# Two stages joined into one block, and a four-bit network whose rounding steps are reordered, in an eight-stage transformer kernel

## What is computed

```python
# layer 0, feed-forward: E = 64 experts, H = 32 hidden, G = 64 tokens a group, K = 16
scores = softmax(xt @ Wr + br)                 # T x E
fs = grouped_routing_scores(scores)            # keeps the best groups of 64 by expert, over all T tokens;
                                               # divided by its sum over the experts + 1e-6
h = silu(up) * gate * fs[:, :, None]           # up, gate: T x E x H
out = einsum('teh,ehd->td', h, Wdown) + fs @ bdown

# layer 1, feed-forward: every 16 neighbours share a scale
def fp4_quant_dequant(x):
    scale = maximum(max(abs(xb)) / 6.0, 1e-12)
    xn = xb / scale
    return nearest_of_grid(xn) * scale         # grid 0, .5, 1, 1.5, 2, 3, 4, 6, with sign
h = silu(fp4(x) @ fp4(w_gate)) * (fp4(x) @ fp4(w_up))      # 352 hidden
out = fp4(h) @ fp4(w_down)
```

## Time and profile before

| | us |
|---|---|
| median of 3 runs (lowest, highest) | 1144.07 (1143.19, 1144.93) |
| the profiled execution | 1143.17 |
| its span in the profile | 1141.1 |
| busy over the span: PE, DVE, ACT, POOL | 884.4, 790.5, 440.5, 128.9 |
| stretch of preparation | 0 to 79 |
| causal attention | 79 to 431.9 |
| route | 431.9 to 671.1, its DMAs to about 677 |
| experts | 681.7 to 859.2 |
| linear attention, layer norm | 859.2 to 953 |
| fp4 network | 953 to 1141.1 |

### The profile page before, as it was taken

The page is one execution under the profiler, slowest core; times in us unless marked ns, Lnnn a source line. Parts: engine busy times, 40 slices in busy tenths (PEclk is TensorE's granted clock), DMA queues, the critical chain, the costliest instruction groups (busy, mean ns, idle before and its releaser), DMA issues. The chain is left out here.

```text
span 1141.1 us, 20063 instructions
## 1 busy us (share of the span) xinstructions
PE 884.4 (78%) x7220; PEld 498.4 (44%) x7220; DVE 790.5 (69%) x1453; ACT 440.5 (39%) x788; POOL 128.9 (11%) x107
## 2 busy tenths in 40 slices
PE   5428999999898766999784719999987974575774
PEld 4116766666565442333231303434435832343442
DVE  0762344688878894999977657888874433899982
ACT  3515666656545333554354620111112264222221
POOL 3420000000000001000005720000000000232232
PEclk8858999999989877999997969999998886787787
DMA  7400000000000000555342347666630000000000
GB/s 187 71 1 2 2 3 2 3 2 3 2 2 2 2 1 37 194 202 185 144 151 109 130 122 238 203 201 200 205 110 1 1 1 0 1 4 15 9 19 28
DMA packets 53988, 79.80 MB, mean 70 GB/s; under 512 B 14288, under 2 KB 28432, under 8 KB 53776
## 3 DMA queue, kind: packets, MB, share of 16 engines
q1 hardware_dynamic: 49520, 76.57, 21.2%
q10 hardware_dynamic: 4384, 2.10, 0.6%
HBM read 40.90 MB, written 35.65 MB: 67 GB/s over the span
## 5 line engine op out<-in xcount | busy, mean ns | idle before, releaser
L1485 PE MATMUL bank<-ex_hh,Wd 128*128 128x512 f32 x256 | 130.3, 601 | 6.7 <-DVE ex_hh L1546 6.7
L1171 ACT ACTIVATE so_u<-bank,bu 128x512 f32<-128x512 f32 x128 | 87.5, 686 | 84.3 <-PE bank L57 84.2
L1546 DVE TENSOR_TENSOR ex_hh<-ex_pg,bank 128x512 f32<-128x512 f32 x128 | 84.4, 674 | 33.4 <-PE bank L1471 16.1
L882 ACT ACTIVATE att_qk<-bank 128x512 f32<-128x512 f32 x128 | 66.8, 602 | 45.2 <-PE bank L712 44.7
L970 DVE TENSOR_TENSOR att_am<-bank,causal 128x512 f32<-128x512 f32 x64 | 44.1, 688 | 50.2 <-PE bank L746 50.1
L746 PE MATMUL bank<-att_qk 64*128 64x128 f32 x1024 | 78.0, 294 | 0.0
L746 PEld LDWEIGHTS bank<-att_qk 64*128 64x128 f32 x1024 | 65.5, 196 | 20.6 <-issue 20.6
L1279 DVE SCALAR_TENSOR_TENSOR so_made<-bank,bg,so_u 128x512 f32<-128x512 f32 x95 | 69.5, 754 | 6.9 <-DMA hidden<-so_made 5.1
L1485 PEld LDWEIGHTS bank<-ex_hh,Wd 128*128 128x128 f32 x256 | 47.9, 192 | 57.0 <-issue 32.7
L1471 PE MATMUL bank<-F,spread 128*128 (+1 forms) x128 | 48.2, 387 | 23.6 <-PEq L122 23.6
L1156 POOL TENSOR_TENSOR so_made<-so_u,so_g 128x512 f32<-128x512 f32 x33 | 44.9, 1396 | 177.0 <-DVE so_cnt L1334 170.2
(11 more groups left out here) (376 smaller groups left out, 1847.6 us busy)
## 6 DMA issues: line engine op xcount, KB each, us to landing
hidden<-so_made SPq DMA_DIRECT2D x128, 256.0 KB, 2.0
ex_pg<-hidden SPq DMA_DIRECT2D x64, 512.0 KB, 4.1
xin<-in_L_attn_x_dram ACTq DMA_DIRECT2D x8, 256.0 KB, 7.0
out_dram<-ff_ot SPq DMA_DIRECT2D x8, 256.0 KB, 2.3
so_other<-so_key SPq DMA_DIRECT2D x2, 512.0 KB, 5.5
wm<-in_L_wmod_dram SPq DMA_DIRECT2D x2, 384.0 KB, 5.0
F<-so_fhi SPq DMA_DIRECT2D x2, 256.0 KB, 4.4
F<-so_flo SPq DMA_DIRECT2D x2, 256.0 KB, 5.7
```

Of the source, the lines that this page charges most:

```text
L882: nc.scalar.activation(qk[t % 2][:, r, :, :].rearrange("p a l -> p (a l)"), psF[r], ACT.Relu).then_inc(s_["fe"], 1)
L1171: nc.scalar.activation(u[m % NU_][:], psU[m % 3][:, :], ACT.Silu, bias=bu[:, k:k + 1], scale=1.0 / WS).then_inc(s_u, 1)
L1485: nc.tensor.matmul(psY[j][:, :], Wd[:, n, :], hh[n % 4][:], start=False, stop=n == EBLK - 1).then_inc(s_dn[n % 4], 1)
L1546: nc.vector.tensor_tensor(hh[k % 4][:], pg[k // 2 % 4][:, k % 2, :], psW[k % 4][:, :], ALU.mult).then_inc(s_hh[k % 4], 1)
```

## The change

**The four-bit helper.** The scale is one scalar_tensor_tensor (max, times 1/6, against a tile `tiny` of 1e-12) in place of a tensor_scalar; the factor 1 - 2^-24 moves from an instruction of its own (old L82) into the division, which becomes a scalar_tensor_tensor. The helper is cut in pieces, so that a stage can place them apart. Where the stage gives one, the maximum is written to PSUM (`mx`).

**fp4_network.** VectorE's turn becomes: divide and round hidden t; gated 0 and 1 of t+1; scales and division of input t+2; gated 2; residual t-1; gated 3; scales of hidden t+1; rounding of input t+2. The last turn's two closing steps run on VectorE, not on GpSimd. PE's turn becomes: gate and up of t+1 (2, 3), input t+3, output t-1, hidden t back (group 0), quantised input t+2 back, hidden group 1, gate and up of t+2 (0), hidden group 2, gate and up (1), down t. In the last turn the three hidden groups go to three banks. The loops of all engines are unrolled.

**route and experts.** `experts` gives back four instruction lists, which are appended to those of `route` in one block; it uses route's buffers. SP waits for the stores, issues the loads of the first two `pg` buffers, sends the first half of the tokens of `F2`, loads the third, sends the second half, loads the fourth. PE waits for the first half before tile 0 and for the second before tile 1. SP's raising of the 30 semaphores of `experts` moves to the start of `route`. ScalarE issues the two `vv` DMAs at n == 20, and PE has six items (was three) ahead of the matmul behind `cg`, two (was three) ahead of the one behind `ends`.

```diff
-def fp4_rounding(nc, step, src, n, w):
...
-    step(nc.vector.tensor_reduce(sc, blocks(src), AX.X, ALU.max, apply_absolute_value=True))
-    step(nc.vector.tensor_scalar(sc, sc, 1.0 / 6.0, 1e-12, ALU.mult, ALU.max))
-    step(nc.vector.reciprocal(rc, sc))
-    step(nc.vector.tensor_scalar(rc, rc, 1.0 - 2.0 ** -24, None, ALU.mult))
-    step(nc.vector.tensor_tensor(blocks(xn), blocks(src), by_block(rc), ALU.mult))
+def fp4_scales(nc, step, src, n, w):
...
+    mx = w.get("mx", sc)
+    step(nc.vector.tensor_reduce(mx, blocks(src), AX.X, ALU.max, apply_absolute_value=True))
+    step(nc.vector.scalar_tensor_tensor(sc, mx, 1.0 / 6.0, w["tiny"][:, 0:n // 16], ALU.mult, ALU.max))
+    return nc.vector.reciprocal(rc, sc)
+
+
+def fp4_divide(nc, src, n, w):
+    return nc.vector.scalar_tensor_tensor(blocks(w["xn"][:, 0:n]), blocks(src), 1.0 - 2.0 ** -24,
+                                          by_block(w["rc"][:, 0:n // 16]), ALU.mult, ALU.mult)
...
+        def experts(sem, u, g, spare, route_done):
...
+            pg = [u[:, 2 * i:2 * i + 2, :] for i in range(4)]
+            hh, rec, y = g[0:4], g[4:6], u[:, 8, :]
...
+                def f2_cols(sp, half):
...
+                    cols = slice(half * W // 2, (half + 1) * W // 2)
+                    for part, src, s in ((0, fhi, s_f), (1, flo, s_fl)):
+                        sp.wait_ge(s, FIRST + half + 1)
...
+                    if eng is nc.sync:
+                        for i in range(NM):
+                            eng.wait_ge(s_store[i], 16 + 16 * (ITEMS // NM))
...
+                        what(0, 0)
+                        what(0, 1)
+                        f2_cols(eng, 0)
+                        what(0, 2)
+                        f2_cols(eng, 1)
+                        what(0, 3)
+                    elif eng is nc.tensor:
+                        if what == 0:
+                            eng.wait_ge(s_u, FIRST + ITEMS)
+                            eng.wait_ge(s_g, FIRST + ITEMS - BY_DVE)
+                        eng.wait_ge(s_f2[what], FIRST + 64)
...
-                            if n == 24:
+                            if n == 20:
                                 act.wait_ge(s_vh, FIRST + 1)
...
-                        up_and_gate(at + 1, at + 4)
+                        up_and_gate(at + 1, at + 7)
                         pe.wait_ge(s_cg, FIRST + 1)
...
-                        up_and_gate(at + 4, at + 7)
+                        up_and_gate(at + 7, at + 9)
                         pe.wait_ge(s_ends, FIRST + 1)
...
+                            if follow > 2:
+                                by_token(t + 3)
+                            if behind:
+                                out_by_token(t - 1)
+                            hidden_back(t, 0, psT)
                             if follow > 1:
                                 quantised_back(t + 2)
...
-                            hidden_back(t)
+                            hidden_back(t, 1, psT if follow > 0 else psH)
                             if follow > 1:
                                 gate_up(t + 2, 0)
+                            hidden_back(t, 2, psT if follow > 0 else psU[0])
+                            if follow > 1:
                                 gate_up(t + 2, 1)
                             down(t)
-                            if behind:
-                                out_by_token(t - 1)
...
+                        def turn(t, follow, behind):
...
                             quantise_hidden(t)
-                            if ahead1:
+                            if follow == 0:
+                                scale_hidden(t)
+                            if follow > 0:
                                 gated(t + 1, 0)
                                 gated(t + 1, 1)
-                            if ahead2:
-                                quantise_x(t + 2)
+                            if follow > 1:
+                                normalise_x(t + 2)
+                            if follow > 0:
+                                gated(t + 1, 2)
                             if behind:
                                 add_x(t - 1)
-                            if ahead1:
-                                gated(t + 1, 2)
+                            if follow > 0:
                                 gated(t + 1, 3)
...
+                                hidden_scales(t + 1)
+                            if follow > 1:
+                                quantise_x(t + 2)
```

More of the change, by code:

```diff
@@ L283, in program @@
             work |= {k: tb("prep_" + k, [P, QW // 16]) for k in ("sc", "rc")}
+            work["tiny"] = tiny
             xin = tb("xin", [P, 8, 4, P])
@@ L1768, in upto, with turns @@
                         eng.wait_ge(s, FIRST + n)
[L1770 removed]
+                def turns(prologue, turn):
                     prologue()
[L1773 to L1777 removed]
+                    for t in range(NT):
+                        turn(t, NT - 1 - t, t > 0)
                 stand(dma=(s_out,))
```

472 lines of the change are left out of this document (243 added, 229 removed).

## The result

The changed kernel takes 1105.01 us (median of 4 runs, 1100.13 to 1107.42) against 1143.63 (4 runs, 1137.07 to 1144.93): ratio 0.9679, 95% interval [0.9646, 0.9712]. Run again, 1101.98, ratio 0.9646 [0.9617, 0.9674]. The forecast was 1116.5 with a range from 1107: right in direction, some 11 to 15 us too little, and outside its range. The profiled execution took 1103.91 with a span of 1102.2, 38.9 less than the span before.

A forecast was written before the change was run, and what follows sets the result against it. VectorE was taken to bound the fp4 network. Network -18.1, join -9.3, vv 0 and preparation +1.0 sum to -26.4 us: 1116.8 from the profiled 1143.17, 1117.7 on the median's scale, stated as 1116.5, range 1107 to 1126.

The forecast's parts named there:

- step 3: Last turn of the fp4 network: closing steps on VectorE, three banks and a faster down product, -4.7 us in sum.
- step 5: Route: vv DMAs issued earlier, but VectorE's chain still ends with GpSimd's work, priced at 0 (ends -3.7 and +1.5).
- step 6: Preparation: the division waits for GpSimd in place of the removed instruction, and reordering costs +1.0 us (ends -0.6 and +1.6).
- The network's middle: Middle fp4 turns: a ring through TensorE takes 16.1 us at full clock, 17.8 with 3.5 us at half clock.
- Rival B: Fp4 network: TensorE keeps full clock, turns of 16.1 us, total 1104 to 1108; chance 0.13.
- The start: Ahead of the network's first turn: earlier transposes of tile 1 and fewer small instructions, -1.5 us (0 to -4).
- The join: Route to experts: scores sent in halves let the product of block k = 3 come earlier, -10.8 us (-7.5 to -11.7).
- the change of stage: Start of route: raising 30 more semaphores at 0.05 us each costs +1.5 us (ends 0 and +3).
- The turns: Six network turns with an input to quantise, each 2.0 us shorter: -12.0 us (ends -21 and +4).
- step 1: Network turns: VectorE's stalls by GpSimd go with the helper's scale tensor_scalars, 4.18 us a turn, leaving VectorE 15.6.
- the move's price: Last turn: tile 6's residual (0.75) and output transposes (1.1) now come ahead of the hidden transposes, +1.8 us.
- Rival E: Route: the earlier vv DMAs carry through to the end, total 1113 us; chance 0.07.

The follow-up runs named there:

- run 5: Changed kernel plus twelve unused fp32 128x160 matmuls in TensorE's idle time in each of six network turns: 1095.86 us, ratio 0.9586.
- run 9: Changed kernel plus unused matmuls wherever TensorE idles throughout the fp4 network, first and last turns and prologue included: 1091.62 us, ratio 0.9567.
- Run 11: Changed kernel with all block maxima of the fp4 network in SBUF, not PSUM; profiled once: scale instruction 1.15 us in place of 0.19.
- run 12: Changed kernel with the scale instruction a tensor_scalar again, its maxima in PSUM in middle turns; profiled once: scale instruction 0.19 us.
- 8: Changed kernel with the last turn's two closing steps on GpSimd again; profiled once: network's end 20.1 us in place of 16.6.
- run 3: Kernel before with only route, experts and the vv DMAs as changed; helper and network as before: 1131.0 us, ratio 0.9881.
- run 7: Changed kernel with the vv transfers issued late again and TensorE's small products in their old places: 1114.81 us in one execution.
- 1: The kernel before, unchanged, measured again: 1143.04 us against 1142.52 on the same chip, ratio 0.9993.
- 13: Changed kernel with the preparation's quantisation in its old form: 1103.61 us, ratio 0.9671.
- 14: Kernel before with only the preparation's quantisation in the new form: 1139.73 us, ratio 0.9992.
- run 4: The changed kernel, unchanged, measured again beside the others on the same chip: 1101.98 us, ratio 0.9646.
- run 15: Changed kernel with the input's rounding right behind its normalising and its two tensor_scalars writing to PSUM: 1091.05 us, ratio 0.9552.

## Why the prediction was right in direction and too small

Three steps failed: the end of the network (step 3, by 2.8 us), the vv transfers (step 5, by 1.8) and the preparation (step 6, by 2.1). Another 7.1 us of the difference between the two profiled executions lie in stages for which the prediction had no term.

**What held.** The network's middle: a ring through TensorE took over from VectorE; 16.1 at full clock predicted, 16.25 measured (run 5); 17.8 a turn with half clock, 17.85 measured. The last is luck in part. Over five turns the mean clock was 0.83, so TensorE had (1 - 0.83) x 2 = 34% of a turn of 17.89 at half, 6.1 us and not the forecast 3.5; the gap ahead of the quantised input was 5.15 and not 3.5 to 4. At the prediction's 0.5 each that would have cost 3.0, and the turn grew by 1.6 over run 5's: more half clock than forecast, and less of it on the ring. Rival B was not what the changed kernel does, but run 5 and run 9 are rival B made true. The start: -1.5, measured -1.5. The join: -10.8 by the product of k = 3, measured 10.75 (17.75 behind the last rounding before, at 688.78, and 7.00 after, at 671.11), and +1.5 for the change of stage, measured +1.8 (last sum onto XT to TensorE's first matmul: 4.56, then 6.35). The turns gave -10.7 for -12.0: I took 19.8 for all six turns before, 118.8, though the working itself had 19.0 for the first, and they were 117.8.

**Right, but for another reason: step 1.** L80's wait went, as forecast. The prediction said so because the new helper has no tensor_scalar in its scale part. Run 11 keeps the new kind of instruction and has the wait back (1.15), run 12 goes back to the old kind and has none (0.19): it was the block maxima in PSUM, which the prediction does not price. No run puts back the hardware loops, TensorE's old order or the shared bank of the last groups one by one; their shares are read from the rows alone.

**Step 3, the end: predicted -4.7, measured -7.5.** Three of its four terms came out: rounding to transposes 4.96 (5.2 by my terms), transposes to down product 3.49 (3.5), down 2.84 (2.9). The down product's 2.84 hangs on the moment at which the clock rose, 1093.2, and runs 5 and 8 show that it can come too late for it. What I left out is the output buffer. Before, tile 6's output left behind the last down product, and the last copy waited 2.54 for its transfer; after, it leaves ahead of it and the last copy waits for nothing but TensorE. From the end of the down product to the end of the span it is 5.3 in place of 7.5. I counted the move's price, +1.8, and not this 2.1. No run tests it alone; the row before names the transfer as what the last copy waited for.

**Step 5, the vv transfers: predicted 0, measured -1.8** (run 3 -1.9, run 7 gives 1.8 back). That the chain ends with GpSimd's work was right: its last product ended at 656.23 and VectorE's instruction beside it at 656.37. The term that failed is what VectorE's instructions add to that work, 10 us in the prediction. The twelve products took 22.50, 7.7 over their 14.8, because three of VectorE's instructions (1.28, 5.36 and 3.08 long) made single products 1.1, 4.1 and 2.0 longer, and little else did. So GpSimd was done 25.5 after the value in place of 27.3 before. Before, that time held an idle of 6.49, which run 7 brings back; it came through ScalarE from TensorE's wait for `cg`. Rival E, priced at the full 3.7, was half right; the scan grew from 4.42 to 5.36 and a TensorE wait of 1.08 came in.

**Step 6, the preparation: predicted +1.0, measured -1.1.** I expected the division to wait in the stead of L82. It ran in 1.33; L76 was held instead, 2.58 to 3.37 us in its profiles, 1.4 to 2.2 less than L82's 4.79. The step that failed is where the wait would fall and how long it would be. The old form moves too: in runs 1, 3 and 13 it is the scale instruction that waits, 4.28 to 5.04. The timed runs cannot tell the whole from nothing (14).

**The rest is the sum's frame.** Step errors make 2.8 (end) + 1.8 + 2.1 - 1.3 (turns) - 0.3 (change of stage) + 0.2 (join) + 0.1 (semaphores in the network, priced but not seen) = 5.4 of the 12.5 us between the forecast of the profiled execution, -26.4, and the 38.9 measured. The other 7.1 lie where nothing was changed: attention 5.3, layer norm 2.2, route up to `so_vv` 0.6, experts 0.2, less 1.2 in the linear attention. Over the profiles attention takes 349.9 to 356.8, the layer norm 25.5 to 27.9 and linear attention 59.5 to 68.2. Their rows differ in TensorE's clock.

Chance in one execution does not explain it all, since the medians gain as much (38.6, and 40.4 in run 4) as the two profiles. The stages also fall into groups. Linear attention and layer norm together take 92.5 to 92.7 in all four profiles without the join; with it they take 84.9 to 85.2 (four), 91.6 to 91.9 (six) or 95.9 to 96.0 (three), 90.6 on average. Attention goes with the form of the preparation (13, 14). So some of these 7 us may be effects of the change that reach stages it does not touch, by the state in which they are entered; that is not shown, and the cause stays open. TensorE in the linear attention, in the changed kernel's second profile and in that of run 7 (same code):

```profile
844.75:904.40 59.65, 51.70 (x360) 0.94 0.00 1
```
```profile
847.12:915.29 68.17, 60.24 (x360) 0.82 0.00 0
```

The first has full clock from 852.3 to the end; in the second the clock fell at 882.7, with TensorE busy in 8.45 of the 10 us ahead, and stayed at half until 899.7. I gave the range only the unknown costs of the edits, and none to the stages behind and ahead of them, which alone move a single execution by 5 or more.

## What to carry to other kernels

When a change shortens an engine's turn, ask which ring is next and at which clock it runs: here it went through TensorE and its idle, and 10 us more lay in filling that idle (run 9) or in handing TensorE its input earlier (run 15). Before pricing a moved transfer at nothing, follow its wait through every list that is worked through in order: here VectorE's wait for it came back to GpSimd by way of one small product in TensorE's list. Against the stalls by GpSimd here, a source or target in PSUM worked whatever the order, and another kind of instruction did not.

## What the runs showed of the hardware

- In the fp4 network a tensor_scalar with both ends in SBUF (2.69 in place of 0.43) and a scalar_tensor_tensor with two SBUF sources (1.15 in place of 0.19) were held until a running GpSimd instruction ended. With one operand in PSUM neither was held (0.19, 0.69, 0.70). In the preparation a scalar_tensor_tensor was let go 1.65 before GpSimd's row ended, and another ran beside it in its usual 1.33.
- Idles of 4.84 and 4.20 us in TensorE were both followed by half clock, but it was full again at 1093.2, ahead of the down product (2.84 us), in one run and at 1088.8, well inside it (4.68), in the other. In the linear attention it fell to half with TensorE busy in 8.45 of the 10 us before in some executions and not in others, worth 8.5 us there.
- Added matmuls with unused results kept the clock at 1.00 over four turns, at 12 fp32 matmuls of 160 columns (3.43 us) a turn.
